# Row operations moved ahead of evacuations in the 512-wide attention, and the decoder attention cut in quarter-head pieces with three float32r products

## What is computed

```python
# layer 2: one attention over 512-wide values
e = s1[:, None] + s2[None, :] + a_b
e = jnp.where(e >= 0, e, 0.2 * e)
e = jnp.where(adj > 0, e, -9e15)
out = jax.nn.softmax(e, axis=1) @ (h @ fc_w + fc_b)

# layer 3: 4 heads of 128, the same attention matrix used twice
att = masked_softmax(adj * sigmoid(f1[:, :, None] + f2[:, None, :]))   # [4, n, n]
Xa = einsum('hij,hjd->hid', att, X @ W)              # encoder attention, then BN + MLP + BN
Y  = einsum('hij,hjd->hid', att, emb)                # decoder attention
Y  = elu(einsum('hnd,hed->hne', Y, W))
out = batchnorm(elu(Y @ dec_W.T + b) + Y)
```

## Time and profile before

| | |
|---|---|
| median of 3 runs | 3566.08 us (3560.08 to 3570.93) |
| profiled execution, its own time | 3560.0 us, span 3558.2 us |
| PE busy | 3160.6 us (89%) |
| PE weight loads busy | 2212.1 us (62%) |
| DVE busy | 2328.3 us (65%) |
| ACT busy | 1715.9 us (48%) |
| POOL busy | 255.4 us (7%) |
| DMA moved | 580.90 MB, 163 GB/s over the span |
| mean granted TensorE clock | 0.953 of full |

### The profile page before, as it was taken

How to read it: one execution, slowest core, us unless ns; L and a number is a source line. 1 busy time by engine, 2 the same in 40 slices (tenths; PEclk the granted TensorE clock), 3 DMA queues, 4 the chain that set the end, 5 groups by cost and what they waited for, 6 DMA issues and landing times. The chain is left out here.

```text
span 3558.2 us, 35485 instructions
## 1 busy us (share of the span) xinstructions
PE 3160.6 (89%) x13715; PEld 2212.1 (62%) x13715; DVE 2328.3 (65%) x3070; ACT 1715.9 (48%) x1553; POOL 255.4 (7%) x441
## 2 busy tenths in 40 slices
PE   5799999999977999975888885999999876999994
PEld 4533333333334777754777774888888736888883
DVE  5599999999864665655666645888888552122226
ACT  0299999999811211113333426888888412000002
POOL 0000000000011111110000000010101000000003
PEclk9999999999998999997999997999999988999997
DMA  7500000000033676666222217676767424766654
GB/s 284 209 17 9 16 16 10 13 15 15 0 107 132 246 273 244 246 224 230 96 98 101 101 68 294 239 282 243 277 244 276 194 72 174 317 272 272 272 201 130
DMA packets 119286, 580.90 MB, mean 163 GB/s; under 512 B 13376, under 2 KB 21795, under 8 KB 95312
## 3 DMA queue, kind: packets, MB, share of 16 engines
q1 hardware_dynamic: 96528, 443.44, 32.8%
q0 software_dynamic: 22592, 135.19, 10.5%
HBM read 374.87 MB, written 203.71 MB: 163 GB/s over the span
## 5 line engine op out<-in xcount | busy, mean ns | idle before, releaser
L516 PE MATMUL bank<-dist,hf 128*65 128x512 f32 (+2 forms) x2112 | 805.1, 543 | 12.4 <-ACT dist L478 12.4
L516 PEld LDWEIGHTS bank<-dist,hf 128*65 128x65 f32 x2112 | 290.6, 138 | 519.0 <-issue 484.2
L1378 PE MATMUL bank<-pt,HA 128*128 128x256 f32 x1936 | 505.1, 381 | 4.5 <-DMA HA<-features 4.5
L478 ACT ACTIVATE dist<-dist 128x1408 f32<-128x1408 f32 (+1 forms) x352 | 452.9, 1322 | 4.6
L1567 PE MATMUL bank<-w,EM 128*128 128x256 f32 x1936 | 426.0, 380 | 12.3 <-DMA w<-weights 12.3
L1567 PEld LDWEIGHTS bank<-w,EM 128*128 128x128 f32 x1936 | 369.3, 191 | 62.6 <-DMA w<-weights 12.5
L1378 PEld LDWEIGHTS bank<-pt,HA 128*128 128x128 f32 x1936 | 328.7, 191 | 28.0 <-DMA HA<-features 4.7
L409 DVE TENSOR_TENSOR dist<-msk,sB 128x1408 f32<-128x1408 uint8 (+1 forms) x208 | 324.9, 1562 | 23.5 <-PE bank L516 13.8
L1366 PE MATMUL bank<-idt,v 128*128 128x128 f32 x1936 | 302.3, 277 | 40.9 <-ACT v L1252 33.6
L1305 DVE COPY pt<-bank 128x512 f32<-128x512 f32 (+1 forms) x440 | 264.4, 630 | 112.5 <-PE bank L1366 110.6
L469 ACT ACTIVATE dist<-dist,neg_t 128x1408 f32<-128x1408 f32 (+1 forms) x208 | 295.1, 1419 | 60.2 <-DVE dist L409 56.9
(11 more groups left out here) (162 smaller groups left out, 4437.8 us busy)
## 6 DMA issues: line engine op xcount, KB each, us to landing
w<-weights SPq DMA_DIRECT2D x44, 2816.0 KB, 9.8
weights<-pt SPq DMA_DIRECT2D x220, 512.0 KB, 3.8
al<-in_adj_cols SPq DMA_DIRECT2D x22, 1408.0 KB, 8.1
at<-in_adj_tiles SPq DMA_DIRECT2D x22, 1408.0 KB, 8.2
rows<-in_adj_rows SPq DMA_DIRECT2D x22, 1408.0 KB, 6.5
HB<-in_adj_rows POOLq DMA_DIRECT2D x22, 1354.0 KB, 7.6
rows_low<-HB POOLq DMA_DIRECT2D x22, 1354.0 KB, 6.0
rows<-rows_low POOLq DMA_DIRECT2D x22, 1354.0 KB, 8.3
```

The source lines that it names most:

```text
L478: act.activation(d[:, 0:VALID[c]], d[:, 0:VALID[c]], ACT.Exp, scale=-1.0).then_inc(p_ready, 1)
L516: mm = pe.matmul(sums_bank(hh, k)[0:FW, 0:hi - a * P], hf[hh][:, m, :], d[:, a * P:hi], start=(m == 0), stop=(m == T - 1))
L1378: t = pe.matmul(acc_t[n % 2][:, 0:P2], HA[:, m, h * D3:(h + 1) * D3], pt[n % 2][:, m, :, :].rearrange("p r n -> p (r n)"), start=(m == 0), ...
```

## The change

In the 512-wide attention, the lists of the engines are written in another order. On DVE, `leaky` of tile j+2 now opens the loop body and `masked_max` follows the first evacuation; `result` of j-1 comes after the third, `missing` of tile j+3 after the fifth, and `xw_out` works one tile later (j-2). On ACT, `z` opens the body, `expo` comes after the third evacuation and the turned tile of the last layer norm after the fifth. On PE, the two parts of `tail` move from after groups 2 and 4 to after groups 4 and 5. On SP, the rows of tile j+1 are asked for ahead of `xin` of tile j, and the load of the values starts after the first two row tiles.

In the encoder's end, each tile is now kept as a float32r copy `EH` (ACT) and a rest `EL` (DVE, after ACT).

In the decoder, a head's weights come in four pieces of 6, 6, 5 and 5 blocks through five buffers. ACT makes a float32r copy of a piece (`split`, four buffers `whi`), DVE writes the rest over the piece itself (`rest`), and PE runs three float32r products for each block in place of one float32 product. `riB` is loaded for each head. The MLP quarter follows the first piece of a head.

```diff
@@ 512-wide attention, SP, ACT, DVE, PE @@
+                    def mask_rows(j):
+                        wait(sp, max_ready, j - 1)
+                        sp.dma_start(rows[j % 2][:, :], adj_rows[j]).then_inc(rows_in[j % 2], 16)
...
-                            wait(sp, max_ready, j - 1)
-                            sp.dma_start(rows[q][:, :], adj_rows[j]).then_inc(rows_in[q], 16)
+                            if j > 1 and j + 1 < T:
+                                mask_rows(j + 1)
                             wait(sp, r_full, 2 * T + j - 1)
                             sp.dma_start(xin[q][:, :], xs[1][j]).then_inc(x_in[q], 16)
...
+                            if j + 2 < T:
+                                z(j + 2, q)
                             for g in range(NG):
                                 if j + 1 < T:
                                     keep_hi(j + 1, g)
-                                if g == 0 and j + 2 < T:
-                                    z(j + 2, q)
-                                if g == 3 and j > 0:
+                                if g == 2 and j + 2 < T:
+                                    expo(j + 2, q)
+                                if g == 4 and j > 0:
                                     tail(j - 1, 1 - q)
-                            if j + 2 < T:
-                                expo(j + 2, q)
...
+                            if j + 2 < T:
+                                leaky(j + 2, q)
                             for g in range(NG):
...
-                                if g == 0 and not head:
+                                if g == 0 and j + 2 < T:
+                                    masked_max(j + 2, q)
+                                if g == 1 and j > 1:
+                                    xw_out(j - 2, q)
+                                if g == 2 and j > 0:
                                     result(j - 1, 1 - q)
-                                if g == 1 and ahead:
-                                    missing(j + 2, i + 1, q)
-                                if g == 2 and ahead:
-                                    leaky(j + 2, q)
-                                if g == 4 and ahead:
-                                    masked_max(j + 2, q)
-                                if g == 5 and not head:
-                                    xw_out(j - 1, 1 - q)
+                                if g == 4 and j + 3 < T:
+                                    missing(j + 3, (j + 3) // 2, 1 - q)
...
-                                if g == 2 and not head:
+                                if g == 4 and not head:
                                     tail(j - 1, 1 - q, 0)
-                                if g == 4 and not head:
+                                if g == 5 and not head:
                                     tail(j - 1, 1 - q, 1)
@@ encoder's end @@
-                            if t % 2:
-                                act.wait_ge(em_mm, t + 1)
-                                act.activation(EM[:, t, :], bank[t % 8][:, :], ACT.Copy).then_inc(em_act, 1)
+                            act.wait_ge(em_mm, t + 1)
+                            act.activation(EH[:, t, :], bank[t % 8][:, :], ACT.Copy).then_inc(em_act, 1)
...
+                            dve.wait_ge(em_act, t + 1)
+                            dve.tensor_tensor(EL[:, t, :], bank[t % 8][:, :], EH[:, t, :].bitcast(FP32), ALU.subtract)\
+                                .then_inc(em_dve, 1)
@@ decoder @@
-            RING = 4
-            w = [sb(ph, f"w{k}", [P, T, P2]) for k in range(RING)]
+            PIECES = [(0, 6), (6, 12), (12, 17), (17, T)]
+            NPC = len(PIECES)
+            WS, HS = 5, 4
+            w = [sb(ph, f"w{k}", [P, 6, P2], F32R) for k in range(WS)]
+            whi = [sb(ph, f"whi{k}", [P, 6, P2], F32R) for k in range(HS)]
...
+                            if k >= WS:
+                                sp.wait_ge(piece_done, k - WS + 1)
+                            sp.dma_start(w[k % WS][:, 0:b - a, :].bitcast(FP32), weights[n][:, a:b, :]).then_inc(w_in[k % WS], 16)
...
+                        pe.wait_ge(wlo_ready, k + 1)
+                        into = acc_t[n % 2][:, 0:P2]
+                        for m in range(a, b):
+                            hi, lo = whi[k % HS][:, m - a, :], w[k % WS][:, m - a, :]
+                            pe.matmul(into, EH[:, m, h * D3:(h + 1) * D3], hi, start=(m == 0), stop=False)
+                            pe.matmul(into, EH[:, m, h * D3:(h + 1) * D3], lo, start=False, stop=False)
+                            t = pe.matmul(into, EL[:, m, h * D3:(h + 1) * D3], hi, start=False, stop=(m == T - 1))
+                        t.then_inc(piece_done, 1)
...
+                    def split(k):
+                        a, b = PIECES[k % NPC]
+                        act.wait_ge(w_in[k % WS], 16 * (k // WS + 1))
+                        if k >= HS:
+                            act.wait_ge(piece_done, k - HS + 1)
+                        act.activation(whi[k % HS][:, 0:b - a, :], w[k % WS][:, 0:b - a, :].bitcast(FP32), ACT.Copy)\
+                           .then_inc(whi_ready, 1)
...
+                    def rest(k):
+                        a, b = PIECES[k % NPC]
+                        dve.wait_ge(whi_ready, k + 1)
+                        dve.tensor_tensor(w[k % WS][:, 0:b - a, :], w[k % WS][:, 0:b - a, :].bitcast(FP32),
+                                          whi[k % HS][:, 0:b - a, :].bitcast(FP32), ALU.subtract).then_inc(wlo_ready, 1)
...
                     for n in range(HEADS):
-                        first(n)
+                        if n > 0:
+                            first(n - 1)
+                        rest(NPC * n + 3)
+                        if n > 0:
+                            first_end(n - 1)
+                        if n + 1 < HEADS:
+                            rest(NPC * n + 4)
                         if n >= H3 + 1:
                             second((n - 1) // H3 - 1, (n - 1) % H3)
-                        first_end(n)
+                        if n + 1 < HEADS:
+                            rest(NPC * n + 5)
+                            rest(NPC * n + 6)
```

More of the change, by code:

```diff
@@ L971, in _ @@
                         keep(0, g)
+                    missing(2, 1, 0)
                     def body(i):
@@ L1405, in build @@
         tail = ExitStack()
-        EM = sb(tail, "EM", [P, T, D])
+        EH, EL = sb(tail, "EH", [P, T, D], F32R), sb(tail, "EL", [P, T, D], F32R)
         PART_PAIRS = (2, 2, 3, 4)
@@ L1560, in _, with attend @@
                 def _(pe):
-                    def attend(n):
-                        h, k = n % H3, n % RING
-                        pe.wait_ge(w_in[k], 16 * (n // RING + 1))
-                        if n >= 2:
+                    def attend(n, x):
+                        h, k = n % H3, NPC * n + x
+                        a, b = PIECES[x]
+                        if x == 0 and n >= 2:
                             pe.wait_ge(at_ready, n - 1)
-                        for m in range(T):
-                            t = pe.matmul(acc_t[n % 2][:, 0:P2], EM[:, m, h * D3:(h + 1) * D3], w[k][:, m, :],
-                                          start=(m == 0), stop=(m == T - 1))
-                        t.then_inc(att_done, 1)
+                        pe.wait_ge(wlo_ready, k + 1)
[6 more added lines that the diff above has]
+                        t.then_inc(piece_done, 1)
                     def mul(p, f):
@@ L1582, in _ @@
                     for n in range(HEADS):
-                        attend(n)
-                        if n == 0:
-                            pe.wait_ge(dw_in, 16)
-                        if n >= H3 + 1:
-                            mul((n - 1) // H3 - 1, (n - 1) % H3)
+                        for x in range(NPC):
+                            attend(n, x)
+                            if n == 0 and x == 0:
+                                pe.wait_ge(dw_in, 16)
+                            if x == 0 and n >= H3 + 1:
+                                mul((n - 1) // H3 - 1, (n - 1) % H3)
                     mul(PAIRS - 2, KT - 1)
@@ L1601, in second @@
                         n = KT * p + f
-                        act.wait_ge(z_done, n + 1)
+                        act.wait_ge(z_done, M1 + n + 1)
                         if n >= 2:
-                            act.wait_ge(s_ready, n - 1)
+                            act.wait_ge(s_ready, M1 + n - 1)
                         act.activation(e2[n % 2][:, :], z_t[n % 2][:, 0:P2], ACT.Exp, bias=mlp_b[:, 1, f:f + 1])\
                            .then_inc(e_ready, 1)
+                    for k in range(HS - 1):
+                        split(k)
                     for n in range(HEADS):
-                        first(n)
+                        split(NPC * n + 3)
+                        if n > 0:
+                            first(n - 1)
+                        if n + 1 < HEADS:
+                            split(NPC * n + 4)
                         if n >= H3 + 1:
```

(22 more changed lines are left out.)

59 lines of the change are left out of this document (28 added, 31 removed).

## The result

The changed kernel takes 3455.5 us (median of 4 runs, 3451.1 to 3464.2), the kernel before beside it 3568.5 us. The ratio is 0.9693 with a 95% interval from 0.9675 to 0.9712: 3.1% faster, 110 us by the ratio and 113 by the medians, where 147 were forecast. The time lies near the top of the stated range of 3390 to 3458.

A forecast was written before the change was run, and what follows sets the result against it. PE was taken to bound the decoder and, with waits for ACT's exponential, the 512-wide attention. Gains 73 + 73 + 3 - 2 = 147 us off 3560.0 gave 3413, as median 3419; stated range 3390 to 3458, the forecast's own 3392 to 3446.

The forecast's parts named there:

- The attention: 512-wide attention: PE's wait for the exponential and the slow clock go; tile 22.84 to 19.2 us, 73 us gained.
- the row loop: 512-wide attention: loop through SP, DMA and DVE, 18.8 us a tile; as rival pacing the stage, 3453 us, 11%.
- The price of a product: Decoder on PE: a 256-column float32r product costs 0.119 us, its weight load hidden.
- The forecast's head of 9.58 us: Decoder on PE: 66 products at 0.119 us, 7.85, plus the MLP quarter's 1.73.
- the rivals of 0.111 and 0.19: Decoder products: cheaper at 0.111 us, 3399 us in all (7%); weight load not hidden at 0.19, 3626 us (5%).
- The step that failed: Decoder's start: a 768 KB piece lands after about 4.3 us, between 2.6 for 256 KB and 6.5 for 1408 KB.
- The sum of the ring: Decoder's five buffers: issue 0.4, landing 4.3, `split` 1.5, `rest` 1.76, products 2.1: 10.1 us; five pieces last 12.0.
- the cover is 1.3 us thick; each further us costs 44: Decoder: DVE ends `rest` of the next head's first piece near +8.3 us; PE wants it at +9.6.
- the first rival: Decoder paced by DVE or the ring of pieces: 10.5 us a head, 37 us gained less, 3456 us; 12%.
- 30% of the DMA rate stands free: Decoder: argument against DVE or the ring of pieces pacing it; 315 GB/s needed, the prefetch ran at 430.
- The rest of the decoder's shortfall: Decoder's heads: forecast 413 us for the stretch, 39 heads of 9.58 and 5 of 7.85, 72.6 less than before.
- The encoder's end and the start: Encoder's end: 2 us lost to ACT's copies; decoder's start: PE's wait 7.6 us in place of 11, 3 gained.

The follow-up runs named there:

- ring of six: The changed kernel with six buffers for the weight pieces in place of five, `u1` sharing `e1`'s memory: 3426.6 us, ratio 0.9609.
- spread products: The changed kernel, five buffers, with the four MLP products one behind each piece of a head, not all behind the first: 3428.8 us, ratio 0.9613.
- The light transfers: The changed kernel, but from the 16th piece on only a piece's first block is transferred, engine work unchanged: 3429.2 us (one run).

## Why the prediction missed

**The attention, right.** Forecast 73 us by 19.2 us a tile; measured 19.1 a tile, 79 us over the stage in the traces and 73 by the ratio of the run of this part alone (77 by its medians). The wait for the exponential is gone and so is the lower clock; DVE waits for its rows as before and PE doesn't: it lacks 3 us of 419, so the row loop, put at 18.8 us, doesn't pace it.

**The price of a product, right.** 0.119 taken, 0.12 measured; the load of 128 columns, 0.19 us long in its records, stays hidden under 256 float32r columns. The forecast's head of 9.58 us is what PE takes when it is hardly kept waiting: 9.58 in the ring of six, 9.51 with the products spread as well, so the last digit is luck. PE's records 0.12 apart also leave no room for the rivals of 0.111 and 0.19. Two sums of the forecast are off without consequence here: at 0.115 a product the decoder gains 84 us, not 87, and its own range would be about 3404 to 3443 where 3392 to 3446 stands.

**The step that failed** is in the decoder's start and was carried over to the ring: "Between 2.6 us for 256 KB and 6.5 for 1408 KB it lands after about 4.3". That is the landing of a piece that is alone in the queue. In the ring, a piece is mostly asked for while two others are under way, in half the cases with a `riB` as well, and the medians are 6.9 and 5.5 us, 6.2 on the mean.

The sum of the ring, 10.1 us against 12.0, doesn't give the loss even with the mean landing. Its 0.4 for the issue stands inside the landing already, so it becomes 6.2 + 1.5 + 1.76 + 2.1 = 11.6, still under 12.0. The wait comes from the piece that is worst placed. In the trace the first piece of a head lands in 7.2 us (median), `split` takes 1.5 and `rest` 1.76, 10.4 together, and its buffer comes free only one head ahead, 9.58 us. A head then takes 10.33. `rest` starts 0.03 us (median) after `split` for this piece, so DVE's order doesn't hold it back. The same sum is 9.5 us with `riB` on the other queue and 9.6 with spread products (with a wait of 0.4 for DVE), where a head takes 9.98 and 9.74.

The forecast's other figure for the same piece, "the cover is 1.3 us thick; each further us costs 44", would give (1.9 - 1.3) x 44 = 26 us with the mean landing, and 39 x (10.33 - 9.58) = 29 were lost; since it counts DVE's order, that is an agreement in size. So the first rival came about, by its half on the ring, and near its price (10.5 a head; 10.33 measured). That its 3456 is within 1 us of the 3455.5 measured is partly luck: the decoder gained 46 us less than forecast where the rival had 37, and the attention more than its 73. "30% of the DMA rate stands free", which spoke against it, was true and beside the point: what counts is when a piece is asked for, not how many a second can be moved. That the ring and not the rate was short is shown by the sixth buffer; that even releases shorten the landings, by the spread products.

**The rest of the decoder's shortfall.** Forecast 72.6, measured 26.6, 46 less. 29 are the 39 heads above. Heads 1 to 4, with no MLP, were put at 7.85 and take 10.16: 4 x 2.3 = 9. There the ring has less time than in the other heads, since no MLP quarter lengthens a head on PE. With six buffers it is 9.08; what keeps that above 7.85 no run takes apart. The light transfers don't tell more of these heads, since their first 15 pieces were whole. The first head takes 15.3 in place of 7.85: 7.5. Its 18 first products stand 0.21 us apart at a granted clock of 0.50, the lower level, after PE had stood idle for 9.65 us (1.7 us more than at 0.12), and behind them PE stands 2.3 us, of which 1.9 are a wait for `dw`:

```profile
2922.40:2926.20 3.80, 3.80 (x18) 3.80 (x18) 3.72 (x3) 2.59 (x3) 0.00 (x0) 0.50 0.68 259
```

The row is the stretch of those 18 products; PEclk, third from the end, is the clock. The head's products end at 2934.5. Its `first` starts 3.2 us later, since in DVE's list it stands behind the rests of three pieces of the next head, the last of which lands at 2935.0. In all 29 + 9 + 7.5 = 46 (rounded).

**The encoder's end and the start, right in size.** From the first issue of weights to the first product it is 8.0 us where it was 11.0, the 3 that were forecast. From the 22nd division to that issue it is 859.3 us where it was 855.8: 3.5 lost where 2 were forecast, with all that lies between. In the other runs with the new encoder's end that stretch takes 858.1 to 862.7 us, so the 3.5 are no firm number.

## What to carry to other kernels

Before a product is made cheaper, cost the ring that feeds it with the landing time of a transfer that has its neighbours in the queue, not of one alone, and do it for the piece that is worst placed, not for the mean: the time from the release of its buffer to its use must exceed queued landing and preparation. Where the sum is close, one more buffer took more off here (0.75 us a head) than a `rest` of a quarter of its length (0.45), and so did an even release (0.59): spread a block of other work on the consuming engine between the pieces rather than leave it in one place. And an average share of free bandwidth didn't tell of it: with five buffers the queue moved 287 GB/s, with six 310, on the same transfers.

## What was not expected of the hardware

- A `riB` of 128 KB, broadcast to 128 partitions, delays the piece behind it by more than its bytes. I took the pieces that were issued over 3 us before the one ahead of them landed. The second of a head lands 1.88 us behind the first (median of 36), 418 GB/s for its 786 kB. The first of a head, which has a `riB` ahead of it, lands 3.33 us behind its predecessor (39); with `riB` on GpSimd's queue 2.00 (37). So it costs 1.3 us, and at the pieces' rate its bytes would take 0.3.
- DMA's busy share is 0.86 for 287 GB/s and was 0.68 for 268 GB/s. What also differs is the packets: 31146 for 131.1 MB in the decoder now, 7735 for 130.1 MB before. The busy share doesn't measure the bytes alone. That the packets' number makes the difference is a reading; no run varies it alone.
